# Chunk 1's value and receptance projections from inputs mixed on GpSimd, and the head's steps in a new order

## The reference: an RWKV block and a gated feed-forward layer

```python
xx = shift(x, 1)                                  # the step before, zero ahead of the first
xk, xv, xr = (x * mix + xx * (1 - mix) for mix in (mix_k, mix_v, mix_r))
k, v, sr = xk @ Wk.T, xv @ Wv.T, sigmoid(xr @ Wr.T)
# a recurrence over the steps, for each channel, with a running maximum pp:
y = (e1 * aa + e2 * v) / (e1 * bb + e2)           # aa, bb: decayed sums of exp(k)*v and exp(k)
x = layernorm(x + (sr * y) @ Wo.T)
h = silu(x @ wg.T) * (x @ wu.T)                   # hidden width 768, int32 weights / 127
out = layernorm(x + h @ wd.T)
```

## Time and profile before

| | |
|---|---|
| time, median of 3 runs | 291.53 us (291.45 to 291.97) |
| time of the profiled execution | 293.12 us |
| its span | 291.3 us |
| mean granted TensorE clock | 0.993 |
| busy: TensorE, VectorE, ScalarE, GpSimd | 275.1, 261.3, 215.2, 189.3 us |

### The profile page before, as it was taken

The page is one execution under the profiler, slowest core; times in us unless marked ns, Lnnn a source line. Parts: engine busy times, 40 slices in busy tenths (PEclk is TensorE's granted clock), DMA queues, the critical chain, the costliest instruction groups (busy, mean ns, idle before and its releaser), DMA issues.

```text
span 291.3 us, 4269 instructions
## 1 busy us (share of the span) xinstructions
PE 275.1 (94%) x1262; PEld 199.9 (69%) x1262; DVE 261.3 (90%) x449; ACT 215.2 (74%) x386; POOL 189.3 (65%) x153
## 2 busy tenths in 40 slices
PE   8999978889999999999999999999999999999990
PEld 5645555646794689658885689468965889688880
DVE  4967899899999999999999999999999999888662
ACT  3596977489766986698956986798769890897472
POOL 3606999979968865986678675887567570353040
PEclk9999999999999999999999999999999999999997
DMA  7900500220103102220204020300220020102003
GB/s 239 366 7 12 208 1 0 73 71 3 36 2 88 58 0 72 65 81 0 72 4 144 0 72 0 77 31 0 72 73 0 1 74 0 36 2 73 0 6 110
DMA packets 13525, 16.26 MB, mean 56 GB/s; under 512 B 704, under 2 KB 11200, under 8 KB 13504
## 3 DMA queue, kind: packets, MB, share of 16 engines
q1 hardware_dynamic: 12816, 15.48, 16.4%
q10 hardware_dynamic: 688, 0.53, 0.6%
HBM read 11.81 MB, written 4.19 MB: 55 GB/s over the span
## 4 chain that ended last, share of the span: by engine, by line
PE 73%; DVE 12%; ACT 7%; issue 3%; POOL 1%; DVEq 0%; POOLq 0%; ACTq 0%
PE bank_b L1077 12%; PE bank_a L1077 12%; PE bank_a L1100 11%; PE bank_b L1045 9%; PE bank_a L1008 7%; PE bank_c L1008 6%; PE bank_d L1008 6%; PE bank_c L982 2%; PE bank_b L1054 2%; DVE stats L758 1%; DVE rwkv L751 1%; POOL wts L364 1%; ACT L576 1%; DVE state L711 1%; PE bank_c L1077 1%
## 5 line engine op out<-in xcount | busy, mean ns | idle before, releaser
L384 POOL TENSOR_TENSOR hlo<-hid,hhi 128x512 fp32r<-128x512 f32 (+1 forms) x36 | 53.3, 1487 | 32.4 <-ACT hhi L554 32.3
L364 POOL TENSOR_SCALAR wts<-gap,par 128x512 f32<-128x512 f32 (+1 forms) x18 | 35.3, 1959 | 25.6 <-DVE gap L679 24.8
L1100 PE MATMUL bank_a<-wd_r,hhi 128*128 128x256 f32 x192 | 47.2, 287 | 1.0 <-POOL hlo L384 0.9
L1100 PE MATMUL bank_a<-wd_r,hlo 128*128 128x256 f32 x192 | 45.8, 279 | 0.0
L478 ACT ACTIVATE mix<-dx,par 128x512 f32<-128x512 f32 x48 | 31.4, 711 | 19.0 <-POOL dx L344 19.0
L350 POOL TENSOR_TENSOR mix<-mix,xt 128x512 f32<-128x512 f32 (+1 forms) x36 | 40.7, 1166 | 0.3 <-ACT mix L478 0.3
L1100 PEld LDWEIGHTS bank_a<-wd_r,hhi 128*128 128x128 f32 x192 | 36.0, 188 | 3.5 <-issue 2.6
L1100 PEld LDWEIGHTS bank_a<-wd_r,hlo 128*128 128x128 f32 x192 | 36.0, 188 | 0.3 <-issue 0.2
L554 ACT ACTIVATE hhi<-hid 128x512 fp32r<-128x512 f32 (+1 forms) x54 | 31.0, 576 | 6.2 <-DVE hid L804 6.2
L804 DVE TENSOR_TENSOR hid<-bank_b,act 128x512 f32<-128x512 f32 (+1 forms) x48 | 30.8, 643 | 3.5 <-issue 1.1
L470 ACT ACTIVATE wts<-wts 128x512 f32<-128x512 f32 (+1 forms) x54 | 27.9, 578 | 7.1 <-DVE wts L688 6.9
(11 more groups left out here) (114 smaller groups left out, 587.2 us busy)
## 6 DMA issues: line engine op xcount, KB each, us to landing
xrow<-x SPq DMA_DIRECT2D x7, 512.0 KB, 3.8
xt<-xT SPq DMA_DIRECT2D x6, 513.0 KB, 3.8
out<-y_buf SPq DMA_DIRECT2D x6, 512.0 KB, 2.8
wg_i<-wg SPq DMA_DIRECT2D x1, 768.0 KB, 8.2
wu_i<-wu SPq DMA_DIRECT2D x1, 768.0 KB, 9.7
wd_i<-wd SPq DMA_DIRECT2D x1, 768.0 KB, 11.4
out<-y_buf SPq DMA_DIRECT2D x3, 256.0 KB, 2.1
xt<-xT SPq DMA_DIRECT2D x2, 257.0 KB, 2.9
```

Of the source, the lines that this page charges most:

```text
L364: nc.gpsimd.tensor_scalar(wts[:, OUT, h, 0:n], gap[:, h, 0:n], par[:, FIRST, h:h + 1], CAP, ALU.add, ALU.min).then_inc(out_arg_ready, 1)
L384: nc.gpsimd.tensor_tensor(hlo[:, m, 0:n], hid[:, m % NH, 0:n], hhi[:, m, 0:n].bitcast(f32), ALU.subtract).then_inc(hlo_ready, 1)
L1100: mm = nc.tensor.matmul(ffn[:, q, :], hp.bitcast(f32) if full else hp, w[:, m, :], start=(m == 0 and q % 2 == 0 and part is hhi), stop=(m ...
```

## The change

All edits lie in the head and in what chunks 1 to 3 need:

- Chunk 1 takes only K in two passes (`project_k1`). Its V and R inputs are mixed on GpSimd (`mixing1`, four instructions) and go through the ordinary `project`.
- TensorE does chunk 0's output product right behind K, then V and half of R, the flag's matmul, and the other half of R. Nothing of chunk 1 is left within round 1.
- ScalarE inverts chunk 0's denominator ahead of the scaling for V and R and of five of the six range checks; one check goes further up, between two exponentials. The checks write to `res2` and no longer to `y_buf`. Round 1 takes the receptance behind its first silu.
- GpSimd casts the gate weights behind chunk 0's numerator, mixes chunk 1's V and R, makes chunk 1's third arguments, and then casts the other two weights.
- VectorE's scans of the denominator's sum for chunk 1 stand ahead of the low parts of x1, not behind.
- Chunk 2's transposed input is loaded to `y_buf` without a wait, chunk 3's to `xt`. Chunk 2's R is mixed behind round 1's `rwkv`, chunk 3's V and R behind the third arguments of chunk 2, where before only R was.
- The wait for the cast down weights moves from ahead of round 1 to the down product.

```diff
             def load_xt(c):
-                if isinstance(c, int) and c == 2:
+                if isinstance(c, int) and c == 3:
                     sp.wait_ge(last_steps_done, 1)
-                elif isinstance(c, int) and c == 3:
-                    sp.wait_ge(squares_ready, 6)
-                elif isinstance(c, int) and c == 4:
-                    sp.wait_ge(mixed, 3 * CH)
-                elif not (isinstance(c, int) and c == 1):
+                    sp.wait_ge(mixed1, 2 * CH)
+                elif not (isinstance(c, int) and c < 3):
                     sp.wait_ge(mixed, (c - 2) * (3 * CH))
...
+            def mixing1(i, h):
+
+                pool.wait_ge(dx_scaled, i * CH + h + 1)
+                nc.gpsimd.tensor_tensor(mix[:, 1, i, h, :], mix[:, 1, i, h, :], xt[:, h, 0:N],
+                                        ALU.add).then_inc(mixed1, 1)
...
                 if j == 1:
-                    mix_chunk(2, 0, [K, R])
+                    mix_chunk(2, 0, [K])
                 if not last(j):
                     carry_state(j + 1)
                 if ahead:
                     pool.wait_ge(rwkv_ready, j + 1)
+                    if j == 1:
+                        mix_chunk(2, 0, [R])
                     diffs(j + 2)
-                    mix_chunk(j + 2, s, [K, V] if j == 1 else range(3))
+                    mix_chunk(j + 2, s, [K] if j == 1 else range(3))
...
                 if j == 1:
-                    mix_chunk(3, s, [R])
+                    mix_chunk(3, s, [V, R])
...
             weights(0, 0)
-            weights(0, 1, range(2))
+            weights(0, 1, [IN_NEW])
+            range_check(0, 0)
+            weights(0, 1, [IN_OLD])
             scale_chunk(1, 1, [K])
             weights(0, 1, [OUT])
             receptance(0)
             sc.preload_act_table_set("natural_log_exp_and_others")
-            scale_chunk(1, 1, [V])
-            range_check(0, 0)
-            range_check(0, 1)
             log_den(0)
             reciprocal(0)
+            scale_chunk(1, 1, [V, R])
+            range_check(0, 1)
             range_check(1, 0)
             range_check(1, 1)
             range_check(2, 0)
             range_check(2, 1)
-            scale_chunk(1, 1, [R])
+            rstd(0, mv1, lnv1, rstd1, mv1_ready, lnv1_ready, rstd1_ready)
             first_norm(0, True)
...
                 if first(j):
                     running_max(1, 0)
                     running_max(1, 1)
-                    range_flag()
                     norm_stats1(0)
                     gaps(1, 0)
+                    exp_args(1, 0)
+                    gaps(1, 1)
+                    exp_args(1, 1)
+                    range_flag()
                     shift_rows1(0)
                     wide_flag()
-                    gaps(1, 1)
-                    exp_args(1, 0)
-                    exp_args(1, 1)
+                    scan_bb(1, 0)
+                    new_kv(1, 0)
+                    scan_bb(1, 1)
                     x1_low(0, 0)
                     x1_low(0, 1)
-                    begin_recurrence(1)
+                    new_kv(1, 1)
                     return
...
                 if first(j):
-                    project_last_step(K)
-                    project_change(K)
-                    project_last_step(R)
-                    project_last_step(V, [0])
+                    project_k1()
                     pe.wait_ge(wo_in, 16)
                 if not last(j):
                     attention_out(j)
                 if first(j):
+                    project(1, 1, V)
+                    project(1, 1, R, [0])
...
-                    project_last_step(V, [1])
-                    project_change(V)
+                    project(1, 1, R, [1])
```

More of the change, by code:

```diff
@@ L245, in xt_of @@
         def xt_of(c):
-            return xt3 if isinstance(c, int) and c == 3 else xt
+            return xt2 if isinstance(c, int) and c == 2 else xt
         def x1_of(c):
@@ L433, in _ @@
             carry_max(1)
[L434 to L438 removed]
+            carry_state(1)
+            convert(wg_r, wg_i, wg_in, wg_ready)
+            mixing1(V, 0)
+            mixing1(V, 1)
+            mixing1(R, 0)
+            mixing1(R, 1)
             out_arg(1, 0)
@@ L561, in round_ @@
                     silu(j - 1, m)
-                    if m == 0 and not (isinstance(j, int) and j == 1):
+                    if m == 0:
                         receptance(j)
@@ L573, in round_ @@
                         hid_high(j - 1, m - 1)
-                    if m == 1 and isinstance(j, int) and j == 1:
-                        receptance(j)
                 sc.preload_act_table_set("natural_log_exp_and_others")
@@ L590, in first_norm @@
             def first_norm(j, nxt):
-                rstd(j, mv1, lnv1, rstd1, mv1_ready, lnv1_ready, rstd1_ready)
+                if first(j):
+                    weights(1, 0, range(2))
+                else:
+                    rstd(j, mv1, lnv1, rstd1, mv1_ready, lnv1_ready, rstd1_ready)
                 norm1(j)
@@ L594, in first_norm @@
                     rstd(j - 1, mv2, lnv2, rstd2, mv2_ready, lnv2_ready, rstd2_ready)
-                if nxt:
+                if first(j):
+                    weights(1, 0, [OUT])
+                    weights(1, 1, range(2))
+                elif nxt:
                     weights(j + 1, 0, range(2))
@@ L598, in first_norm @@
                 x1_high(j, 1)
-                if nxt:
+                if first(j):
+                    weights(1, 1, [OUT])
+                elif nxt:
                     weights(j + 1, 0, [OUT])
@@ L990, in project @@
                     pe.wait_ge(mixed0, before + 1)
+                elif isinstance(c, int) and c == 1:
+                    pe.wait_ge(mixed1, CH if i == V else 2 * CH)
                 else:
@@ L1010, in project, with project_k1 @@
                     mm.then_inc(ready, 1)
[L1012 to L1014 removed]
+            def project_k1():
                 pe.wait_ge(xt_in, 16)
[L1016 to L1031 removed]
+                pe.wait_ge(gap_ready, CH)
                 for d in range(CH):
                     for h in range(CH):
[L1034 to L1035 removed]
+                        mm = nc.tensor.matmul(bank_a[:, d, :], wkT[:, h, d * P:(d + 1) * P], xt[:, h, 0:N],
+                                              start=(h == 0), stop=False)
+                mm.then_inc(last_steps_done, 1)
+                for d in range(CH):
+                    for h in range(CH):
+                        pe.wait_ge(dx_scaled, h + 1)
+                        mm = nc.tensor.matmul(bank_a[:, d, :], wkT[:, h, d * P:(d + 1) * P], mix[:, 1, K, h, :],
                                               start=False, stop=(h == CH - 1))
[L1037 removed]
+                    mm.then_inc(k_ready, 1)
             def attention_out(c):
```

57 lines of the change are left out of this document (18 added, 39 removed).

## The result

The changed kernel takes 295.64 us, median of 4 runs (295.37 to 296.42), beside 291.73 us for the kernel before in the same session (291.45 to 291.97, 4 runs). The ratio is 1.0129, 95% interval 1.0108 to 1.0150: slower by 3.8 us. The prediction was 291.7 us, with 293.2 us as the upper end of its range. (The two rivals that were slower had been priced at 293.5 and 293.4 us, beyond that end.) Both gates that it named are late.

A forecast was written before the change was run, and what follows sets the result against it. Bound: TensorE, entering its unbroken stretch through two gates set by GpSimd and VectorE taking turns. Late -2.1 + 0.55 + 2.0 = +0.45, early -2.7 + 0.55 + 2.0 = -0.15, middle +0.15 on 291.53: 291.7 us, range 290.0 to 293.2.

The forecast's parts named there:

- Both gates that it named: The end of rwkv in round 1, at 52.61 us before, and the low part of tile 4 in round 2.
- TensorE in the head: Head: two of six passes go, 6.9 us of work; gains only what the other engines let it.
- the late one: Head: GpSimd's cast of the gate weights takes its turn before chunk 0's rwkv, which then ends at 20.4 us.
- V's projection in round 1: Round 1, TensorE: V's projection, 3.43 us, and three down tiles fit before rwkv's end at 50.5 us.
- The clock as a rival at 0.04: Round 1: TensorE idle, clock falls from 2.4 to 1.2 GHz, V's projection 3.4 us longer; 293.4 us, chance 0.04.
- The casts behind the third arguments: Head to round 1: up and down weights' casts delay chunk 2's differences to 33.75 us late or 33.15 early, against 32.61.
- the turn chain: VectorE's operations on two SBUF inputs and GpSimd's work take turns, about 1.0 to 1.1 us each.
- Round 1's turn chain: First difference to rwkv's end, 20.0 us before: three turns leave, 3.25 us less; rwkv ends 2.1 or 2.7 us earlier.
- Behind rwkv: Round 1 after rwkv: R's mixings ahead of chunk 3's differences delay ScalarE's scalings and VectorE's shift; cost 0.55 us.
- Round 2: Third arguments to tile 4's low part: chunk 3's V adds two mixings, two turns, to a full chain; cost 2.0 us.
- the late case: Whole sum if the cast goes before chunk 0's rwkv: -2.1 + 0.55 + 2.0 = +0.45 us.
- The rival that GpSimd comes too late into round 1: Casts make scans wait, chunk 2's differences begin at 35.2 us, rwkv gains 0.6; sum +1.95, 293.5 us; chance 0.25.

The follow-up runs named there:

- e1: Changed kernel with four filler products on zeros behind K of chunk 1: 294.95 us, ratio 1.0099.
- e4: Kernel before with TensorE held behind K of chunk 1 until chunk 0's rwkv is there: 296.42 us, ratio 1.0136.
- e2: Changed kernel with chunk 3's V mixed ahead of chunk 2's third arguments, as before: 293.47 us, ratio 1.0047.
- e12: e11 without any filler: 291.90 us, ratio 0.9988.
- e5: Kernel before with chunk 3's V mixed together with R, behind chunk 2's third arguments: 294.07 us, ratio 1.0069.
- e3: Changed kernel with the gate weights' cast held until chunk 0's rwkv is written: 294.36 us, ratio 1.0083.
- e6: Changed kernel with the edits of e1, e2 and e7 together: 292.51 us, ratio 1.0014.
- e7: Changed kernel with nine filler products in round 1 alone, four ahead of the last gate and up tile, five ahead of down tile 2: 294.17 us, ratio 1.0080.
- e11: e10 with chunk 3's differences ahead of chunk 2's R mixings in round 1: 291.15 us, ratio 0.9961.
- e9: e6 with chunk 2's R mixed ahead of round 1's rwkv, as in the kernel before: 292.34 us, ratio 1.0007.
- e8: e6 with the up weights' cast ahead of chunk 1's third arguments: 292.05 us, ratio 1.0002.
- e10: e8 and e3 together, with two fillers behind K and two ahead of down tile 2: 292.03 us, ratio 0.9999.

## Why the prediction was wrong

**TensorE in the head: the step that failed first.** The prediction let TensorE idle behind K at no cost ("This gains only what the other engines let it") and gave the output product no term: its sum has the residual start right behind the two maxima, at 22.8, which asks for a product that is done by then. The product took 3.39 us and ended at 23.80. Of its two cases for `rwkv`, the late one came true to 0.14 us (20.26 against 20.4). From there the head without the fall is as predicted: third arguments at 25.09 in e1 against 25.3. With the fall they are at 26.50.

**V's projection in round 1: the step that cost most.** The prediction had it and three down tiles done before `rwkv`. It took 5.08 us at half clock, and the output product waited 2.1 us behind `rwkv`.

**The clock as a rival at 0.04.** What it described came about (idle time, a fall, a slower V), and nearly in its place in round 1 (TensorE idle 41.49 to 43.35 and 45.67 to 47.53, predicted 42.5 to 45). V's projection took 5.08 us instead of 3.6, where 3.4 us more had been reckoned. The fall in the head it didn't have. It was given 4 in 100 because no stretch of before showed a fall while work was left. That was an argument from a kernel whose gaps on TensorE are at most 1.20 us there; it had no row on what happens after an idle of 2 us. The Trainium skill, page "TensorE: Matmul & The Clock Gate", Part 1, cited in the prediction for just this, has the clock fall when the engine was idle. In the head e1 and e4 agree (gap of 0.64 us, no fall; 3.26 us, a fall); the gaps of 2.24 us (e2) and 2.27 us (e12) without a fall, and e5's fall behind the gaps of the kernel before, show that the length of one gap doesn't tell it.

**The casts behind the third arguments.** Predicted start of chunk 2's differences 33.75, measured 35.90: 1.20 from the later third arguments, 0.27 because these took 4.41 us instead of 4.14, and 0.69 because the copy of the maxima fell behind the whole first scan (1.21 us, where 0.55 was counted). With the clock up in the head it is 34.39 to 34.49. TensorE waits 0.95 us for the up weights' cast, up to 33.69, and 0.98 us for the flag, up to 30.20 ("about half a microsecond"); neither touches the turn chain.

**Round 1's turn chain: right.** The prediction took 3.25 us off the 20.0 between the first difference and `rwkv`'s end. Measured: 52.92 - 35.90 = 17.02 us, and 17.02 to 17.07 in e1, e2, e3, e6, e7, e11 and e12; 20.0 in e4 and e5, which have the order of before. e9, with one turn more, has 18.15, which makes 1.1 us of R's mixing and 1.9 of the two scans. e8 and e10 have 17.97 and 17.96, since their first difference begins before the second product with v is done; e10 and e11 have the same program up to here, so a start alone can shift a turn across the line. The term is 3.0 us. Since it is the same with the clock down, `rwkv`'s lateness (+0.31 instead of -2.1) is from its start in 2.15 of 2.4 us. The output product came later still, +2.35, because of V's projection at half clock: 2.1 us of waiting that e2, e6, e7, e11 and e12 don't have, e2 and e12 without a filler in round 1.

**Behind rwkv: +0.55, right where `rwkv` sets the end.** In the changed kernel the output product is late by itself and hides the mixings of R, hence -0.58. In e7, the same order with the output product on time, it is 10.09 us from `rwkv`'s end to the third arguments in place of 9.53: +0.56. There `shift` ends 8.21 us behind `rwkv`'s end, predicted 8.2: ScalarE's scalings end late, `shift` waits 1.05 us for `rstd`, and the second maximum waits behind `shift`. With V mixed ahead of the third arguments (e6, e8, e10) the term is 1.3 us, 0.75 more, because `shift` then takes 0.91 us instead of 0.16. e11 takes 1.05 us of that away by one exchange. For this reason mending the clock alone gives less than it shows: the output product of e7 is 3.38 us earlier than in the changed kernel, of which 1.0 is given back here (third arguments 2.39 us earlier).

**Round 2: +2.0, measured +2.26**, and 2.27 and 2.28 us in the same stretch of e2 and e5. Right, as was the place: four mixings ahead of the denominators. But these began at 75.44, not near 70.4, since the round began late.

**The sum again.** Predicted -2.1 + 0.55 + 2.0 = +0.45; measured +2.35 - 0.58 + 2.26 = +4.03. In e7, with the clock up in the head and from 40 us on, the same three are -1.19 + 0.57 + 2.27 = +1.65: even so 1.2 us above the late case, of which 0.6 are the later start of the differences. The turn arithmetic that the prediction spent most of its words on was sound. The rival that GpSimd comes too late into round 1 (from a start of 33.9 on) was met as well: at 35.90, and at 34.45 with the clock up, where `rwkv` gains 1.1 us, half of what the sum had.

**What stays open.** Why a fall comes in one place and not in another: e12's 2.27 us gap and e2's 2.24 had none, e5 fell behind gaps of 1.19 and 0.39 us, and the second fall stood at 44 to 51 us in some executions and at 30 to 39 in others of nearly the same code. That fillers help in round 1 is shown by e7; that they do so by ending the idle time is the likeliest reading, not shown, since the falls move even where the code is the same. With one profile of each kernel, an execution's fall and the median of its runs can't be tied together.

## What to carry to other kernels

Taking work off a full TensorE can make the kernel slower, if the work covered a wait: look for each new gap (here 1.92 us) and ask what the next products cost at half clock. Where VectorE and GpSimd take turns, count the turns between two fixed points; here that came within 0.3 us, and was the same to 0.05 us in eight kernels; in two others (e8, e10) a shifted start added a turn of 0.9 us. A gain at one gate is only worth what the next gate lets through, so redo the sum from the moved point on, with the order in which the next chunk's producers are fed (differences first, since ScalarE waits for them, then what TensorE needs last).
